# The carried state of a chunked linear attention: one full 128x128 product, or four tiled products per pair of heads

## The reference

```python
def step(Sst, qkv):
    qb, kb, vb = qkv
    attn = jnp.einsum('bihd,bjhd->bhij', qb, kb) * causal
    intra = jnp.einsum('bhij,bjhe->bihe', attn, vb)
    inter = jnp.einsum('bihd,bhde->bihe', qb, Sst)
    Sst = Sst + jnp.einsum('bjhd,bjhe->bhde', kb, vb)
    return (Sst, intra + inter)
```

## Time and profile before

| | |
|---|---|
| median of 3 runs | 1115.26 us |
| lowest, highest | 1110.68, 1119.51 us |
| span of the profiled execution | 1185.4 us |
| attention loop in it | about 150 to 720 us |
| PE, DVE, ACT, POOL busy | 88%, 76%, 54%, 44% of the span |

### The profile page before, as it was taken

One profiled execution on the slowest core, in us unless ns is written; L12 is line 12 of the kernel. 1 busy time (PEld: TensorE's weight loads), 2 busy tenths in 40 slices (PEclk: granted clock), 3 DMA queues, 4 the chain that ended last, 5 costly groups with the idle time before them and its releaser, 6 DMA issues.

```text
span 1185.4 us, 26150 instructions
## 1 busy us (share of the span) xinstructions
PE 1044.6 (88%) x8982; PEld 766.7 (65%) x8982; DVE 901.3 (76%) x2067; ACT 643.1 (54%) x1580; POOL 519.2 (44%) x480
## 2 busy tenths in 40 slices
PE   4775788889998898999999997989998899899997
PEld 3553556656676665666766665767776677677774
DVE  3785577789995677778878787788888887886764
ACT  2432444445564555766657554756666566555564
POOL 2216144431324443222232126767886554465552
PEclk9798899999998999999999899999999899999999
DMA  8994233332333332222222116331532233225230
GB/s 231 399 343 102 72 98 113 106 97 87 107 103 96 92 102 80 72 69 69 71 75 70 49 37 178 92 96 27 152 101 63 65 96 107 54 78 151 80 90 18
DMA packets 85504, 124.16 MB, mean 105 GB/s; under 512 B 11264, under 2 KB 68096, under 8 KB 81280
## 3 DMA queue, kind: packets, MB, share of 16 engines
q1 hardware_dynamic: 75136, 97.30, 27.4%
q0 software_dynamic: 10240, 25.18, 7.5%
HBM read 71.32 MB, written 51.13 MB: 103 GB/s over the span
## 4 chain that ended last, share of the span: by engine, by line
PE 57%; DVE 21%; ACT 9%; issue 7%; another core or an unknown queue 4%; SPq 0%; DMA 0%; POOL 0%; DVEq 0%; ACTq 0%; POOLq 0%
PE wide L1437 7%; PE bank L1412 7%; PE bank L1497 6%; PE bank L1699 5%; PE bank L1689 5%; PE wide L1689 5%; DVE epp L1775 4%; PE bank L1481 4%; DVE kvw L1782 3%; PE bank L1489 2%; PE bank L1426 2%; DVE att L1539 2%; PE bank L1399 2%; ACT epp L1750 1%
## 5 line engine op out<-in xcount | busy, mean ns | idle before, releaser
L1652 POOL TENSOR_TENSOR kvw<-kvw,hq 128x512 f32<-128x512 f32 x128 | 171.7, 1341 | 150.5 <-ACT kvw L1742 150.3
L907 POOL DMA_INDIRECT gst<-attended_rows,idxs x128 | 136.7, 1068 | 211.5 <-DVE att L1539 107.5
L1539 DVE SCALAR_TENSOR_TENSOR att<-reach,endrel,wide 128x1024 f32<-128x1024 f32 x152 | 194.5, 1279 | 37.7 <-PE wide L1437 20.9
L258 POOL DMA_INDIRECT routed_rows<-hq,idxs x128 | 127.7, 998 | 216.3 <-DVE att L1539 108.0
L1775 DVE TENSOR_TENSOR epp<-kvw,epp 128x512 fp32r<-128x512 f32 x160 | 144.4, 903 | 77.7 <-ACT epp L1750 75.5
L1699 PE MATMUL bank<-epp,w2p 128*128 128x512 f32 x480 | 163.2, 449 | 7.0 <-DVE epp L1775 6.7
L1750 ACT ACTIVATE epp<-kvw 128x512 fp32r<-128x512 f32 x160 | 100.7, 630 | 95.6 <-DVE kvw L1782 91.3
L1689 PE MATMUL bank<-hp,w1p 128*128 128x512 f32 x480 | 139.8, 400 | 0.0
L1689 PE MATMUL wide<-hp,w3p 128*128 128x512 f32 x480 | 137.6, 395 | 0.0
L1412 PE MATMUL bank<-kvw,turned 128*128 x304 | 132.4, 518 | 3.7 <-ACT turned L1302 1.6
L1437 PE MATMUL wide<-turned,kx 32*128 32x128 f32 x2432 | 113.8, 300 | 18.6 <-DVE att L1539 12.7
(11 more groups left out here) (267 smaller groups left out, 1876.3 us busy)
## 6 DMA issues: line engine op xcount, KB each, us to landing
hq<-weight_rows SPq DMA_DIRECT2D x16, 2048.0 KB
rows<-routed_rows SPq DMA_DIRECT2D x76, 256.0 KB
routed_rows<-zero SPq DMA_DIRECT2D x2, 7168.0 KB, 33.2
attended_rows<-ob SPq DMA_DIRECT2D x76, 128.0 KB
routed_rows<-zero SPq DMA_DIRECT2D x1, 5120.0 KB, 16.6
out<-fin SPq DMA_DIRECT2D x16, 256.0 KB, 2.5
routed_rows<-hq,idxs POOLq DMA_INDIRECT x128
gst<-attended_rows,idxs POOLq DMA_INDIRECT x128
```

What stands on the lines that cost most here:

```text
L258: pool.indirect_dma_start(hs[s], bass.IndirectOffsetOnAxis(idxs[:, t, k:k + 1], 0), hq[:, t, :], None, bounds_check=BLOCKS[s] * P - 1, oob ...
L907: pool.indirect_dma_start(gst[:, u, k, :], None, orow[s], bass.IndirectOffsetOnAxis(idxs[:, t, k % TOPA:k % TOPA + 1], 0), bounds_check=BL ...
L1539: dve.scalar_tensor_tensor(out=att[:, n % 2, :, :], in0=reach[:, :, :].rearrange("p a c -> p (a c)").unsqueeze(1) .to_broadcast([P, 4, 2 * ...
L1652: pool.tensor_tensor(g, g, rows_of(1 - b % 2, n, n + 1), ALU.mult).then_inc(s_eu, 1)
```

## The change

A partition of the state holds one feature of one head; of its 128 columns only 16 are ever different from zero. The change keeps 32 columns instead, those of the pair of heads that share a strip of 32 partitions. A new constant `pairm` takes the place of `headm` in the masking: it is `parity`, which says for each partition whether its head is the even or the odd one of its pair, copied over 16 columns each. The state product is made as four products, each with the 32 keys of a pair of heads as stationary columns and the 32 value columns of the same pair as moving ones, into the 32 partitions of the pair. The application is four products too, each from the 32 partitions of a pair to the 32 partitions of the same pair, with 128 moving columns. mask_states and sum_state work on 32 columns. Semaphores and their counts are the same: the last of the four products signals.

```diff
+        pairm = sb("pairm", [P, 2, DK])
...
+                    link(dve.tensor_copy(pairm[:, :, :], parity[:, :].unsqueeze(2).to_broadcast([P, 2, DK])))
...
-        sh = tb("sh", [P, 2, P])
-        kf, km, qm, sm = (hq[:, 4 * i:4 * i + 4, 0:D] for i in range(4))
+        sh = tb("sh", [P, 2, 2 * DK])
+        kf, km, qm = (hq[:, 4 * i:4 * i + 4, 0:D] for i in range(3))
+        sm = hq[:, 12:16, 0:2 * DK]
...
-                pe.matmul(bank[1][:, 3 * P:4 * P], km[:, m % 4, :], vx[:, m % 6, :, 0:DK], start=True,
-                          stop=True).then_inc(s_st, 1)
+                for p in range(4):
+                    mm = pe.matmul(bank[1][32 * p:32 * p + 32, 3 * P:3 * P + 2 * DK],
+                                   km[:, m % 4, 32 * p:32 * p + 32], vx[:, m % 6, 2 * p:2 * p + 2, 0:DK],
+                                   start=True, stop=True)
+                mm.then_inc(s_st, 1)
...
-                pe.matmul(bank[2][:, n % 2 * P:(n % 2 + 1) * P], sm[:, (n + 3) % 4, :], qm[:, n % 4, :],
-                          start=(n % 2 == 0), stop=True, skip_group_check=True)
+                for p in range(4):
+                    r = slice(32 * p, 32 * p + 32)
+                    pe.matmul(bank[2][r, n % 2 * P:(n % 2 + 1) * P], sm[r, (n + 3) % 4, :], qm[r, n % 4, :],
+                              start=(n % 2 == 0), stop=True, skip_group_check=True)
...
-                dve.tensor_tensor(sh[:, m % 2, :], bank[1][:, 3 * P:4 * P], headm[:, :],
-                                  ALU.mult).then_inc(s_sh, 1)
+                dve.tensor_tensor(sh[:, m % 2, :], bank[1][:, 3 * P:3 * P + 2 * DK],
+                                  pairm[:, :, :].rearrange("p a d -> p (a d)"), ALU.mult).then_inc(s_sh, 1)
```

## The result

On the chip of the comparison the changed kernel took 1104.64 us (1100.83 to 1111.20, 18 runs) beside 1113.91 us (1109.81 to 1121.52, 18 runs) for the one before: ratio 0.9926, 95% interval 0.9906 to 0.9946. On a chip of another kind, on which the kernel before takes 1189 us, it is slower: 1.0119 (1.0080 to 1.0159). The first profile of before, with its span of 1185.4 us, was of that second kind; the three runs beside it were of the first. I call them the 1114 us kind and the 1189 us kind.

A forecast was written before the change was run, and what follows sets the result against it. The prediction took the attention loop as bound mainly by TensorE; +6 (oTs waits) + 2 (other iterations) - 5 (mask-decided) = +3 us, put on the 1115.26 us median: 1118 us, range 1100 to 1143.

The forecast's parts named there:

- my +0.02: TensorE in some 83 iterations of the attention loop: carried's 0.12 less states' 0.10, +0.02 us each, +2 us in all.
- my signs of being wrong: Even iteration of 3.05 us moving over 0.1 us, carried's eight passes over 0.4 us, or mask's chain share and loop falling.
- The term for states: Attend's first load to keys_values' first pass, 0.90 us before: between -0.15 and +0.01 us, taken as -0.10.
- No wait is added: Attention loop: states' waits are the old ones and the work queued behind them is the old work, so no cost.
- The term for carried: Last transpose to scores: 0.42 us becomes 0.54 with four 32*32 tiles, +0.12 us per iteration, bounds -0.08 and +0.78.
- who feels it: Loop iterations split: 48 waiting for oTs, +6 us; some 83 others, +2 us; about 21 decided by the mask, -5 us.
- 48 that wait for oTs: Iterations where turn_outputs waits for ScalarE's copy oTs: states' gain is waited away, carried's +0.12 stays, +6 us.
- VectorE's relief: mask_states and sum_state on 32 columns: 0.24 us together per iteration, almost all hidden, -5 us from 21 iterations.
- The first rival: Scores' wait for the mask: VectorE sets the pace in half of the 152 iterations, -14 us, 1101 us; chance 0.15.
- turning point: Number of iterations decided by VectorE from which the sum turns to a gain: some 27, at 0.24 us each.
- Slower by issue: TensorE's queue: 24 more loads and passes per iteration delay keys_values, states +0.1, carried +0.15, +28 us, 1143; chance 0.19.
- One bank: Carried's four row tiles on bank 2 run one after the other, 0.66 us more, +89 us, 1204 us; chance 0.07.

The follow-up runs named there:

- full application: Changed kernel with the application one full product again, from a 128-column state copy spread by GpSimd: 0.9872 (1114 us kind), 0.9887 and 0.9897 (1189 us kind) against before.

## Why the prediction was wrong

**The reading of TensorE was right, pass by pass.** States 0.16 us shorter (0.15 worked out), carried 0.13 to 0.14 longer (0.12), with an idle weight queue of 0.17 and 0.20 us on its two sides. I then took 0.10 for states instead of the 0.15 of my own sum, for caution: undisturbed iterations went from 2.96 to 2.92 us, where my +0.02 had them going up. One of my signs of being wrong came even so, carried's eight passes at over 0.4 us (0.42): it was set too tight.

**The term for states was right in size, partly by luck.** Forecast: -0.10 in 83 iterations, -8 us. Measured -9.8 and -7. TensorE's step is larger and more of it is lost: to the mask, to oTs, and to a register load that I didn't price at all. "No wait is added" was true and missed that a queue instruction that waits for nothing also needs cover. It was 0.33 us long in the trace of before, and hidden.

**The term for carried was too large.** +0.12 on 131 iterations is +16 us; measured +12, +9 and +7. The step that failed is "who feels it", the number of iterations behind each term: 48 that wait for oTs, 21 that the mask decides, 83 others. On the 1114 us kind there are 7, 32 and so 113. Part of carried's extra time disappears in the waits for the mask, and the 48 waits of turn_outputs for oTs, which carried +6 us of my sum, are almost gone. With these counts and my own prices the sum is 7 x 0.12 + 113 x 0.02 - 32 x 0.24 = -4.6 us, and with the 0.15 that I had worked out for states -10 us; -8.2 was measured. The counts alone turn the sign. (This is an estimate made afterwards.)

**VectorE's relief was too small.** -5 us forecast, from the 21; measured -7.0 (-9.9 to -4.0). The two operations gave 0.215 us (the sum of the state got to 254 ns, not 220), and 7.0/0.215 is 33 iterations, about the 32 visible waits of the 1114 us kind. The first rival, "VectorE sets the pace more often than the visible waits say", had the right place and sign, at 0.15, with 76 iterations and 1101 us. That there are more such iterations than visible waits is not shown: the waits were visible, in a profile of the right kind of chip. Its turning point was also off: by its own terms the sum changes sign at 31 iterations, not at 27, where it is still +1 us.

**One cause stands behind these counts.** The profile was of an execution 70 us longer than the runs. I saw that, and put the difference on the median as a constant. It wasn't one: nearly all of it lay in the loop (from first to last scores 568 us in it, 503 us in the profile of before on the other kind: 64 of the 78 us between the two spans), where the waits are from which I counted. On the kind of chip that the profile came from, +14 us was measured and +3 forecast. The sign agrees, but that is no confirmation: the terms of the sum give no 14 us, and what makes them is open.

**The other rivals.** Slower by issue: 28 us had been its price; the queue does hold keys_values, but only in one of four blocks, 9 us. One bank: wrong. Carried's eight passes on bank 2 take 0.42 us, one lasting 0.28, so all start within 0.15 us, the four tiles side by side. The Trainium skill's sentence (TensorEngine Tiling (Array Packing), Gotcha 1: PSUM Pressure) doesn't hold for row tiles that write different partitions of a bank; here the measurement decides.

## What to carry to other kernels

Set the profiled execution's span beside the runs' median first. If they differ by more than the change can bring, the waits in that profile are not those of the runs: profile again before counting who waits. Price a product on TensorE by the shapes before and behind it, since a change of tile shape costs about as much here as a pass (0.20 us from pass to pass over it, 0.11 within a shape); and when something on a queue gets shorter, list what it covered, queue instructions too.

## What the runs showed of the hardware

- Two kinds of chip run the same program in 1114 us (three chips) and in 1189 us (two), with the same pace of passes (undisturbed iterations of before 2.96 us on both). On the slower kind TensorE's signals of scores and attend come late in 94% of the cases in which GpSimd issues an indirect transfer and in 10% of the others (changed kernel 82% and 15%, full application 78% and 8%); on the faster kind in 1 or 2 of 304.
- Eight passes of 32 columns in four 128*32 tiles take 0.24 us with one lasting 0.19, so they start within 0.05 us; eight of 128 columns in 32*32 tiles within 0.15 us.
- A change from full passes to 32*32 tiles makes the step from pass to pass 0.20 us where it was 0.11. The idle time of the weight queue alone is a poor measure of a change: it is 0.17 us before those tiles, 0.20 us behind them, 0.11 us between scores and attend (304.75 + 0.54 to 305.40), 0.04 us between states and keys_values, and 0.18 us, 73 times in the kernel before, between two loads for full-array passes:

```profile
PEld bank L1399 <- issue: 13.3, 73, 0.2
```

- A load of four numbers into registers in TensorE's queue takes 0.33 us, hidden before the change (keys_values waited 3 times, 0.6 us) and in the open after it (35 times, 9 us).
